# Memory layer: weighing in 32-row tiles, the surprise split between VectorE and Pool

## The chip, the cores and the metric

The program runs on one core of a Trainium2 chip. The metric is the device time of one execution in microseconds, as the median of three runs. Engines are named as in the profile: PE (TensorE; PEld are its weight loads), DVE (VectorE), ACT (ScalarE), POOL (GpSimd), SP (SyncE, which here only issues DMAs).

## The reference, cut to what matters

The reference is a stack of eight layers over x of 4 x 1024 x 128 in float32: four mixing layers, each followed by an expert layer. The change is in the seventh, a segment-wise memory attention with 16 heads of 64 and 32 segments of 32 tokens:

```python
def step(carry, inp):                      # one segment, all batches and heads
    mem, z = carry
    scores = where(mask, q_s @ k_s.T * SCALE, -inf)
    sdpa = softmax(scores) @ v_s
    sq, sk = elu1(qn_s), elu1(kn_s)        # q and k before the rotation
    mem_out = (sq @ mem) / (sq @ z + 1e-6)
    out = beta * mem_out + (1 - beta) * sdpa
    prev_v = (sk @ mem) / (sk @ z)
    mem = mem + sk.T @ (v_s - prev_v)      # v_s - prev_v: the surprise
    z = z + sk.sum(tokens)
```

then `out` times w_out is added to x.

## The kernel before, in words

`memory_layer` (L1845) walks 128 items j: 32 segments, and for each segment 4 groups of 4 heads. An item holds all 4 batches: 128 partitions are 4 batches x 32 tokens. Within an item the 4 heads are two pairs (index n or blk), each with an even and an odd head (parity, e).

Each engine has its program written out by hand: one loop over k, and in each round calls for different items, so that the items are pipelined. Engines meet by semaphores alone; each executes its queue in order.

- PE in round k: `score(k-2)` (L2092: q times k rotated), `prev(k-2)` (L2115: keys times memory), `lift_values(k)` (L2127: values of the new item), `weigh(k-4)` (L2104 and L2107), `num(k-2)` (L2120: queries times memory), `lift_keys(k)` (L2175: keys transposed), `project(k+1)` (L2138: q and k of the next item), one `product` (L2149: a finished output times w_out; four rounds make up one addition to x), `learn(k-3)` (L2168: the memory's update).
- DVE in round k: `remember(k-4)` (L2229: update taken off the memory), `sines(k)` (L2235), `cosines(k)` (L2240), `shares`, `scale_p` and `turn_p(k-3)` (L2244, L2248, L2254: softmax divided by its sum and turned over in 32x32 blocks), in every fourth round `add` (L2288), in some rounds row statistics (L2292, L2296), and `recall(k-2)`: scores masked (L2259), 1/z (L2261), maximum (L2263), the surprise as four instructions, one for each head (L2272: previous value times 1/z minus value), 1/denominator (L2275), and the memory's part of the output, `m1` (L2279).
- ACT in round k: `copy_out(k-4)` (L2041: the weighed output out of PSUM), `lift_out(k)` (L2065), `features(k+1)` (L2048, L2049, L2051), `recall(k-2)` (L2058: four exponentials).
- POOL in round k: `features(k)` (L2013), `spread(k-3)` (L2000), `rotate(k)` (L2007). SP sends the sines' product to the neighbouring partitions by two DMAs for each k (L1962, the `mates`); `rotate(k)` waits for them, `cosines(k+1)` waits for `rotate(k)`, since it overwrites its input.

`weigh` adds two things in PSUM: m1 turned over (a product with the identity), and values times probabilities. The four batches share the 128 partitions, so `spread` first lays the probabilities out as a 128x128 matrix for each head, which is zero outside of its batch's 32x32 block and holds the gate (1 - beta): 128x512 elements an item. `weigh` is then 2 matmuls of 128x128 and 4 matmuls of 128 rows by 64 columns, each over 128 columns. A float32 matmul makes two records in the profile. The 128x512 gate table `own_g` is made by POOL before the loop (L1978 to L1989).

`learn(j)` waits for the surprise of j, which `recall(j)` has finished one round before. `remember(j)`, the first of DVE's next round, waits for `learn(j)`.

Of the kernel before, what the change touches and what calls it, by code (L numbers as in the profile page):

```python
# [8 lines left out]
ALU = mybir.AluOpType  # L9
ACT = mybir.ActivationFunctionType  # L10
AX_X = mybir.AxisListType.X

P = 128
# [1831 lines left out]
def memory_layer(nc, g, wq, wk, wv, w_out, ln_g, ln_b, mem_beta, rope):  # L1845
# [11 lines left out]
    PR, NU, SC = 0, PB * E1, 2 * PB * E1  # L1857
    UP, OT = 4, 192
    N = W * NQ
    LEARNED = N - NQ  # L1860
    GROUP = 4 * NQ
    with ExitStack() as ctx:
# [22 lines left out]
        pe_, pn, pt = s.sb("pe_", [P, QH, SEG]), s.sb("pn", [P, QH, SEG]), s.sb("pt", [P, QH, SEG])  # L1885
        pt_e = s.sb("pt_e", [P, 2, QH, BATCH, SEG])
        own, share, own_g = s.sb("own", [P, BATCH, SEG]), s.sb("share", [P, H]), s.sb("own_g", [P, NQ, QH, BATCH, SEG])
        nm, sm, rs = s.sb("nm", [P, QH]), s.sb("sm", [P, 2, QH]), s.sb("rs", [P, QH])
# [5 lines left out]
        b_up = ps[:, UP:UP + BATCH, 0:PB * E1]  # L1894
        b_ot = ps[:, UP:UP + PB, OT:OT + P]
        b_out = ps[:, UP + 2:UP + 4, OT:OT + 2 * P].rearrange("p c (d f) -> p c d f", f=P)

        names = ("rows_loaded", "gate_loaded", "loaded", "made", "g_ready", "setup", "xn_ready", "turned", "xt_ready", "proj_ready", "t2_ready", "mates_even", "mates_odd",
                 "ab_used", "below_ready", "er_ready", "below_exp", "el_ready", "rope_ready", "lift_ready", "lifted", "scored", "recalled", "s1_ready", "rd_ready", "nm_ready",
                 "u_ready", "den_ready", "dn_ready", "m1_ready", "p_ready", "share_ready", "own_gated", "rsum_ready", "pn_ready", "pt_ready", "pte_ready",  # L1900
                 "upd_ready", "mem_ready", "weighed", "ot_copied", "out_ready", "x_ready", "stats")
# [43 lines left out]
        with nc.Block() as block:  # L1945
# [18 lines left out]
            @block.gpsimd  # L1964
            def _(pool):
                nc.gpsimd.memset(mask[:], 0.0).then_inc(S["made"], 1)
                for b in range(BATCH):
                    pool.wait_ge(S["made"], b + 1)
                    nc.gpsimd.affine_select(out=mask[32 * b:32 * b + 32], in_=mask[32 * b:32 * b + 32], compare_op=ALU.is_ge, fill=-1.0e30,
                                            base=0, pattern=[[0, PB], [-1, SEG]], channel_multiplier=1).then_inc(S["made"], 1)  # L1970
                pool.wait_ge(S["made"], 5)
                nc.gpsimd.memset(mem[:], 0.0).then_inc(S["made"], 1)
                pool.wait_ge(S["made"], 6)
                nc.gpsimd.memset(mem[:, :, :, :, D:E1], 1.0e-6).then_inc(S["made"], 1)
                pool.wait_ge(S["made"], 7)
                nc.gpsimd.memset(uu[:, :, :, D:E1], -1.0).then_inc(S["made"], 1)
                pool.wait_ge(S["made"], 8)
                nc.gpsimd.memset(own[:], 0.0).then_inc(S["made"], 1)  # L1978
                for b in range(BATCH):
                    pool.wait_ge(S["made"], 9 + b)  # L1980
                    nc.gpsimd.memset(own[SEG * b:SEG * b + SEG, b, :], 1.0).then_inc(S["made"], 1)
                pool.wait_ge(S["made"], 13)


                pool.wait_ge(S["share_ready"], 1)
                for q in range(NQ):
                    for e in range(2):
                        shape = [P, PB, BATCH, SEG]
                        gated = nc.gpsimd.tensor_tensor(own_g[:, q, e * PB:e * PB + PB], own[:].unsqueeze(1).to_broadcast(shape),  # L1989
                                                        share[:, q * QH + e:q * QH + QH:2].unsqueeze(2).unsqueeze(3).to_broadcast(shape), ALU.mult)  # L1990
                gated.then_inc(S["own_gated"], 1)
                pool.wait_ge(S["own_gated"], 1)

                def spread(j):

                    pool.wait_ge(S["pt_ready"], j + 1)
                    if j >= 2:
                        pool.wait_ge(S["weighed"], j - 1)
                    shape = [P, QH, BATCH, SEG]
                    nc.gpsimd.tensor_tensor(pt_e[:, j % 2], pt[:].unsqueeze(2).to_broadcast(shape), own_g[:, j % NQ], ALU.mult).then_inc(S["pte_ready"], 1)  # L2000

                def rotate(k):
                    if k >= 2:
                        pool.wait_ge(S["scored"], k - 1)
                    pool.wait_ge(S["ab_used"], k + 1)
                    pool.wait_ge(mates_ready[k % 2], 32 * (k // 2 + 1))
                    nc.gpsimd.tensor_tensor(rope_qk[:, k % 2].rearrange("p a b -> p (a b)"), t1[:], mates[:, k % 2, :], ALU.subtract).then_inc(S["rope_ready"], 1)  # L2007

                def features(k):
                    pool.wait_ge(S["below_exp"], k + 1)  # L2010
                    if k >= 3:
                        pool.wait_ge(S["recalled"], k - 2)
                    nc.gpsimd.tensor_tensor(el[:, k % 3].rearrange("p a b -> p (a b)"), ee[:], rr[:], ALU.add).then_inc(S["el_ready"], 1)  # L2013

                for k in range(N + 3):
                    if k < N:
                        features(k)
                    if 0 <= k - 3 < N:
                        spread(k - 3)
                    if k < N:  # L2020
                        rotate(k)

            @block.scalar
            def _(act):
# [11 lines left out]
                def copy_out(j):  # L2036
                    act.wait_ge(S["weighed"], j + 1)
                    w, q = j // NQ, j % NQ
                    if j >= 2 * GROUP and j % GROUP == 0:
                        act.wait_ge(S["out_ready"], 4 * NQ * (j // GROUP - 1))  # L2040
                    nc.scalar.activation(oT[:, w // 4 % 2, q * PB:q * PB + PB, :, w % 4, :], b_ot.rearrange("p n (b t) -> p n b t", t=SEG), ACT.Copy).then_inc(S["ot_copied"], 1)  # L2041

# [35 lines left out]
            def _(pe):  # L2078
# [16 lines left out]
                def weigh(j):  # L2095
# [4 lines left out]
                    if j:  # L2100
                        pe.wait_ge(S["ot_copied"], j)
                    pe.wait_ge(S["pte_ready"], j + 1)
                    for n in range(PB):
                        nc.tensor.matmul(ps[:, UP + n, OT:OT + P], m1[:, j % 2, 2 * n:2 * n + 2, :].rearrange("p h d -> p (h d)"), g.ident[:], start=True, stop=False, skip_group_check=True)  # L2104
                    for n in range(PB):
                        for e in range(2):
                            last = nc.tensor.matmul(ps[D * e:D * e + D, UP + n, OT:OT + P], values_of(j)[:, 2 * n + e, :], pt_e[:, j % 2, PB * e + n].rearrange("p b t -> p (b t)"),  # L2107
                                                    start=False, stop=True, skip_group_check=True)
                    last.then_inc(S["weighed"], 1)
# [31 lines left out]
                def product(k, p, b):  # L2141

                    i, first = parts[p]
                    pe.wait_ge(S["ot_copied"], GROUP * i + 3 * NQ + first // PB + 1)
                    pe.wait_ge(S["mem_ready"], min(k - 3, LEARNED))
# [31 lines left out]

                pe.wait_ge(S["made"], 13)
                for c in range(2 * BATCH):
# [28 lines left out]
            def _(dve):  # L2208
# [8 lines left out]
                dve.wait_ge(S["g_ready"], 1)  # L2217
                dve.wait_ge(S["made"], 13)
                nc.vector.tensor_scalar_add(gate[:, 1:3, :], gate[:, 1:3, :], 1.0).then_inc(S["setup"], 1)
# [30 lines left out]
                def turn_p(j):  # L2250
                    dve.wait_ge(S["pn_ready"], j + 1)
                    if j:
                        dve.wait_ge(S["pte_ready"], j)
                    nc.vector.transpose(pt[:].rearrange("p a b -> p (a b)"), pn[:].rearrange("p a b -> p (a b)")).then_inc(S["pt_ready"], 1)  # L2254

                def recall(j):
# [9 lines left out]
                                                   gate[:, 1, q * QH:q * QH + QH].rearrange("p (k e) -> p e k", e=2), ALU.add, ALU.mult).then_inc(S["den_ready"], 1)  # L2266
                    dve.wait_ge(S["lifted"], j + 1)
                    if 2 <= j < LEARNED:
                        dve.wait_ge(S["upd_ready"], j - 1)
                    for h in range(QH):  # L2270
                        e, n = h // PB, h % PB
                        last = nc.vector.scalar_tensor_tensor(uu[:, r, h, 0:D], prev_view[:, e, n, 0:D], rd[:, h:h + 1], values_of(j)[:, 2 * n + e, :], ALU.mult, ALU.subtract)  # L2272
                    last.then_inc(S["u_ready"], 1)
                    dve.wait_ge(S["den_ready"], j + 1)
# [23 lines left out]
                for k in range(N + 6):  # L2298
                    if 0 <= k - 4 < LEARNED:
                        remember(k - 4)  # L2300
                    if k < N:
                        sines(k)
# [4 lines left out]
                    if 0 <= k - 3 < N:  # L2307
                        scale_p(k - 3)
                        turn_p(k - 3)
                    if k in added_in:  # L2310
                        add(added_in[k])
                    if k - 1 in stats_in:
# [149 lines left out]
```

## Time and profile before

| | us |
|---|---|
| median of 3 runs | 2612.66 (2610.97 to 2617.28) |
| profiled execution: span from first to last instruction | 2623.8 |
| memory layer's loop: first and last L2000 start | 1769.6 and 2440.9 |
| busy over the whole span: PE, PEld, DVE, ACT, POOL | 2176.9, 1549.2, 1700.0, 1437.8, 1106.7 |

The profiled execution's own device time is not given apart from its span; the launch around the span is not in it, and the span alone is already 11.1 us over the median of the runs without a profile. A row of the timeline reads: start, duration, engine, line, operation, output<-input, shapes, how many instructions are merged, and in brackets the idle time in front and what ended it. In a windows row, the busy time of each engine in a stretch stands with its number of records.

### The profile page before, as it was taken

How to read it: one execution, taken by the hardware profiler on the slowest of the kernel's cores; microseconds unless marked ns; L12 is line 12 of the kernel's file. 1: busy time of each engine (PE TensorE's matmuls, PEld its weight loads, DVE VectorE, ACT ScalarE, POOL GpSimd, SP SyncE). 2: the span in 40 equal slices, each digit the busy share in tenths (PEclk: the TensorE clock that was granted, in tenths of full speed). 3: DMA queues.
4: the chain of work that ended last, by engine and by line, in shares of the span. 5: the costliest groups of instructions: out<-in, count | busy, mean ns of one | idle time of the engine just before them, and what ended most of it. 6: DMA issues, size and time to landing. Idle time of an engine off the chain costs nothing. (4 is left out here: it accounts for less than half of the span.)

```text
span 2623.8 us, 79243 instructions
## 1 busy us (share of the span) xinstructions
PE 2176.9 (83%) x30448; PEld 1549.2 (59%) x30448; DVE 1700.0 (65%) x5819; ACT 1437.8 (55%) x3704; POOL 1106.7 (42%) x1076
## 2 busy tenths in 40 slices
PE   6499948589964889899999977948999999999696
PEld 3288845379862233333334336937778777787396
DVE  6722247642336778787878833358999989899522
ACT  5455544355552256455455555537777767776353
POOL 2066644146654120120200004547777777776164
PEclk7699979789986799998989888969999999999798
DMA  4011120011125121111111000121111111111013
GB/s 133 33 42 43 43 85 2 33 32 44 43 93 163 55 58 31 38 39 31 35 46 35 5 33 29 41 85 54 54 53 56 52 53 55 52 56 52 35 42 92
DMA packets 76025, 134.96 MB, mean 51 GB/s; under 512 B 17225, under 2 KB 32264, under 8 KB 73224
## 3 DMA queue, kind: packets, MB, share of 16 engines
q1 hardware_dynamic: 62080, 102.07, 12.6%
q0 software_dynamic: 13568, 27.81, 3.7%
q8 instruction: 250, 4.10, 0.7%
q14 instruction: 119, 0.97, 0.1%
q10 hardware_dynamic: 8, 0.00, 0.0%
HBM read 65.19 MB, written 32.79 MB: 37 GB/s over the span
## 5 line engine op out<-in xcount | busy, mean ns | idle before, releaser
L1544 ACT ACTIVATE ca_pt<-ca_ps 128x512 f32<-128x512 f32 (+3 forms) x768 | 341.1, 491 | 322.3 <-PE ca_ps L1649 137.2
L734 PE MATMUL ffn_ps<-ffn_xst,ffn_up_w 128*128 128x128 f32 x3392 | 420.8, 278 | 0.2 <-issue 0.2
L734 PEld LDWEIGHTS ffn_ps<-ffn_xst,ffn_up_w 128*128 128x128 f32 x3392 | 402.9, 195 | 1.2 <-issue 1.2
L857 DVE TENSOR_TENSOR ffn_hid<-ffn_sg,ffn_ps 128x512 f32<-128x512 f32 x212 | 145.8, 688 | 359.2 <-PE ffn_ps L734 110.9
L576 POOL DMA_INDIRECT ffn_xs<-ffn_x,ffn_token_at x212 | 205.2, 968 | 301.5 <-DVE ffn_token_at L840 165.5
L581 POOL DMA_INDIRECT ffn_y<-ffn_ys,ffn_result_at x212 | 208.8, 985 | 139.2 <-DVE ffn_ys L863 82.3
L1645 PE MATMUL ca_ps<-ca_stacks 75*128 75x512 bf16 (+3 forms) x768 | 245.2, 342 | 18.3 <-ACT ca_pt L1544 10.7
L1777 DVE TENSOR_REDUCE ca_m_far<-ca_ps 128x1 f32<-128x128 f32 (+5 forms) x384 | 236.7, 616 | 30.3 <-PE ca_ps L1623 27.9
L643 ACT ACTIVATE ffn_sg<-ffn_ps 128x512 f32<-128x512 f32 x212 | 125.7, 593 | 233.6 <-remote 182.3
L1623 PE MATMUL ca_ps<-ca_stacks 72*128 72x512 bf16 (+3 forms) x768 | 223.4, 356 | 34.1 <-DVE ca_m_near L1778 21.9
L1778 DVE CUSTOM_DVE_ANT_0 ca_spill<-ca_ps,ca_bias_q 128x256 f32<-128x256 f32 (+1 forms) x512 | 201.1, 397 | 10.9 <-PE ca_ps L1623 10.9
L2000 POOL TENSOR_TENSOR im_pt_e<-im_pt,im_own_g 128x512 f32<-128x512 f32 x128 | 162.9, 1273 | 105.7 <-DVE im_pt L2254 105.7
L2007 POOL TENSOR_TENSOR im_rope_qk<-im_t,im_mates 128x512 f32<-128x512 f32 x128 | 163.1, 1275 | 65.4 <-DMA im_mates<-im_t 58.5
L1468 POOL TENSOR_TENSOR ca_full<-ca_rot 128x512 f32<-128x512 f32 x12 | 15.3, 1277 | 397.9 <-DVEq L1731 397.9
L742 PE MATMUL ffn_ps<-w_w,ffn_hid 128*128 x1136 | 158.0, 282 | 25.3 <-DVE ffn_ys L863 22.0
L2013 POOL TENSOR_TENSOR im_el<-im_ee,im_rr 128x512 f32<-128x512 f32 x128 | 162.9, 1273 | 34.7 <-ACT im_ee L2051 33.5
L1667 PE MATMUL ca_ps<-ca_pt,ca_vp 128*9 128x512 f32 (+3 forms) x1536 | 170.1, 516 | 0.0
L1623 PEld LDWEIGHTS ca_ps<-ca_stacks 72*128 72x128 bf16 x768 | 66.0, 101 | 164.9 <-DVE ca_m_near L1778 100.0
L742 PEld LDWEIGHTS ffn_ps<-w_w,ffn_hid 128*128 128x128 f32 x1136 | 137.7, 191 | 41.6 <-issue 39.9
L1645 PEld LDWEIGHTS ca_ps<-ca_stacks 75*128 75x128 bf16 x768 | 76.3, 100 | 138.3 <-ACT ca_pt L1544 86.3
L2058 ACT ACTIVATE im_pe_<-im_s,im_nm 128x32 f32<-128x32 f32 x512 | 156.9, 315 | 1.9 <-DVE im_nm L2263 1.9
L650 ACT ACTIVATE ffn_up_w<-w_w 128x1024 f32 x142 | 150.4, 1060 | 11.0 <-DVE ffn_table_e L829 3.6
(340 smaller groups left out, 4742.0 us busy)
## 6 DMA issues: line engine op xcount, KB each, us to landing
im_mates<-im_t SPq DMA_DIRECT2D x256, 128.0 KB
ffn_got<-ffn_y SPq DMA_DIRECT2D x48, 256.0 KB, 5.8
ca_stacks<-scratch_q_piece SPq DMA_DIRECT2D x16, 576.0 KB
ca_stacks<-scratch_k_piece SPq DMA_DIRECT2D x48, 192.0 KB
ffn_x<-ffn_xn SPq DMA_DIRECT2D x32, 256.0 KB, 2.0
w_w<-in_L_ffn_experts_w_dram SPq DMA_DIRECT2D x2, 2048.0 KB, 12.0
ffn_xs<-ffn_x,ffn_token_at POOLq DMA_INDIRECT x212
ffn_y<-ffn_ys,ffn_result_at POOLq DMA_INDIRECT x212
```

Of the source, the lines that this page charges most:

```text
L576: nc.gpsimd.indirect_dma_start(out=xs[:, n % XS, :], out_offset=None, in_=xn_rows[:, :], in_offset=bass.IndirectOffsetOnAxis(ap=token_at[: ...
L581: nc.gpsimd.indirect_dma_start(out=y_rows[:, :], out_offset=bass.IndirectOffsetOnAxis(ap=result_at[:, n:n + 1], axis=0), in_=ys[:, n % YS, ...
L734: last = nc.tensor.matmul(ps[:, bank, j * P:j * P + P], up_w[:, n % WS, first + j * P:first + j * P + P], xst[:, n % 2, :], start=True, st ...
L742: last = nc.tensor.matmul(ps[:, 5, 0:P], hid[:, n % 2, j * P:j * P + P], down(e, j), start=(j == 0), stop=(j == IB - 1))
L1544: nc.scalar.activation(pt[:, i % 8, lo - c0:hi - c0], ps[:, tile_bank(i), lo - c0:hi - c0], ACT.Exp, scale=SCALE).then_inc(p_ready, 1)
L1623: last = nc.tensor.matmul(slot_row(n)[:, c:e], stacks[0:KD, u % 3, 0, j, qt * P:qt * P + P], stacks[0:KD, u % 3, 1, j, c:e], start=True, s ...
L1645: last = nc.tensor.matmul(ps[:, tile_bank(i), lo - c0:hi - c0], stacks[:, u % 3, 1, j, kt * P:kt * P + P], stacks[:, u % 3, 0, j, lo:hi], ...
L1667: nc.tensor.matmul(ps[32 * j:32 * j + D + 1, 7, lo - c0:hi - c0], vp[:, b % 2, kt, gr * G4 + j, :], pt[:, i % 8, lo - c0:hi - c0], start=( ...
L1777: nc.vector.tensor_reduce(m_far[:, u % 2, t:t + 1], slot_row(n)[:, 0:lo], AX_X, ALU.max)
L1778: nc.vector.tensor_tensor_reduce(spill[:, n % 2, 0:hi - lo], slot_row(n)[:, lo:hi], bias_q[:, h, W2 - (hi - lo):W2], 1.0, NEG, ALU.add, AL ...
L2000: nc.gpsimd.tensor_tensor(pt_e[:, j % 2], pt[:].unsqueeze(2).to_broadcast(shape), own_g[:, j % NQ], ALU.mult).then_inc(S["pte_ready"], 1)
L2007: nc.gpsimd.tensor_tensor(rope_qk[:, k % 2].rearrange("p a b -> p (a b)"), t1[:], mates[:, k % 2, :], ALU.subtract).then_inc(S["rope_ready ...
```

## The change

1. `weigh`: m1 and the values are no longer used across all 128 partitions. For each pair n there are 8 matmuls with the identity's 32x32 block and 8 matmuls with the probabilities, each of 32 rows (one batch), 64 columns (one head) and 32 columns of data: 32 matmuls an item in the place of 6. The output now lies in four PSUM banks (one a batch) and not in two.
2. `spread` becomes `gate_p`: one 128x128 multiplication by the gate. The table `own_g` and its making fall away; four small copies of the shares take its place. The number that PE and DVE wait for at the start goes from 13 memsets to 8.
3. The surprise: DVE makes previous value times 1/z for all four heads in one instruction (128x256, broadcast); POOL's new `surprise(k-3)`, between `gate_p(k-3)` and `rotate(k)`, subtracts the values in place (128x256) and releases `learn`.
4. `add` moves within DVE's round from behind `turn_p` to behind `remember`; `weigh` waits for it, and `product` waits for the `copy_out` of the same round, since output and products now share two banks.

```diff
+        pt_g = s.sb("pt_g", [P, 2, QH, SEG])
+        share, sorted_share = s.sb("share", [P, H]), s.sb("sorted_share", [P, NQ, QH])
-        b_ot = ps[:, UP:UP + PB, OT:OT + P]
-        b_out = ps[:, UP + 2:UP + 4, OT:OT + 2 * P].rearrange("p c (d f) -> p c d f", f=P)
+        b_ot = ps[:, UP:UP + BATCH, OT:OT + PB * SEG]
+        b_out = ps[:, UP + 2:UP + 4, OUT:OUT + 2 * P].rearrange("p c (d f) -> p c d f", f=P)
...
+                for q in range(NQ):
+                    gated = nc.gpsimd.tensor_copy(sorted_share[:, q]..., share[:, q * QH:q * QH + QH]...)
-                def spread(j):
+                def gate_p(j):
                     pool.wait_ge(S["pt_ready"], j + 1)
                     if j >= 2:
                         pool.wait_ge(S["weighed"], j - 1)
-                    shape = [P, QH, BATCH, SEG]
-                    nc.gpsimd.tensor_tensor(pt_e[:, j % 2], pt[:].unsqueeze(2).to_broadcast(shape), own_g[:, j % NQ], ALU.mult).then_inc(S["pte_ready"], 1)
+                    nc.gpsimd.tensor_tensor(pt_g[:, j % 2], pt[:], bl(sorted_share[:, j % NQ], SEG), ALU.mult).then_inc(S["ptg_ready"], 1)
+                def surprise(j):
+                    pool.wait_ge(S["known"], j + 1)
+                    pool.wait_ge(S["lifted"], j + 1)
+                    new = pairs(uu[:, j % 2, :, 0:D])
+                    nc.gpsimd.tensor_tensor(new, new, sorted_heads(values_of(j)), ALU.subtract).then_inc(S["u_ready"], 1)
...
                     if 0 <= k - 3 < N:
-                        spread(k - 3)
+                        gate_p(k - 3)
+                    if 0 <= k - 3 < LEARNED:
+                        surprise(k - 3)
                     if k < N:
                         rotate(k)
...
                     if j:
                         pe.wait_ge(S["ot_copied"], j)
-                    pe.wait_ge(S["pte_ready"], j + 1)
+                    if adds_by[j + 4]:
+                        pe.wait_ge(S["x_ready"], adds_by[j + 4])
+                    pe.wait_ge(S["ptg_ready"], j + 1)
                     for n in range(PB):
-                        nc.tensor.matmul(ps[:, UP + n, OT:OT + P], m1[...], g.ident[:], start=True, stop=False)
-                    for n in range(PB):
-                        for e in range(2):
-                            last = nc.tensor.matmul(ps[D * e:D * e + D, UP + n, OT:OT + P], values_of(j)[:, 2 * n + e, :], pt_e[...], start=False, stop=True)
+                        heads = [(b, e, slice(SEG * b, SEG * b + SEG), ps[D * e:D * e + D, UP + b, OT + SEG * n:OT + SEG * n + SEG]) for b in range(BATCH) for e in range(2)]
+                        for b, e, tok, out in heads:
+                            nc.tensor.matmul(out, m1[tok, j % 2, 2 * n + e, :], g.ident[tok, tok], start=True, stop=False)
+                        for b, e, tok, out in heads:
+                            last = nc.tensor.matmul(out, values_of(j)[tok, 2 * n + e, :], pt_g[tok, j % 2, PB * e + n, :], start=False, stop=True)
...
-                    pe.wait_ge(S["ot_copied"], GROUP * i + 3 * NQ + first // PB + 1)
+                    pe.wait_ge(S["ot_copied"], min(k - 3, N))
...
-                    dve.wait_ge(S["lifted"], j + 1)
                     if 2 <= j < LEARNED:
                         dve.wait_ge(S["upd_ready"], j - 1)
-                    for h in range(QH):
-                        e, n = h // PB, h % PB
-                        last = nc.vector.scalar_tensor_tensor(uu[:, r, h, 0:D], prev_view[:, e, n, 0:D], rd[:, h:h + 1], values_of(j)[:, 2 * n + e, :], ALU.mult, ALU.subtract)
-                    last.then_inc(S["u_ready"], 1)
+                    nc.vector.tensor_tensor(pairs(uu[:, r, :, 0:D]), prev_view[:, :, :, 0:D], over(rd[:], D), ALU.mult).then_inc(S["known"], 1)
...
                     if 0 <= k - 4 < LEARNED:
                         remember(k - 4)
+                    if k in added_in:
+                        add(added_in[k])
                     if k < N:
                         sines(k)
...
                         turn_p(k - 3)
-                    if k in added_in:
-                        add(added_in[k])
```

## Rows read from the trace of the kernel before

**Rows 1.** Instructions of one tile (the probabilities laid out): duration min/median/max ns, first and last start
```profile
L2000 POOL TENSOR_TENSOR im_pt_e<-im_pt,im_own_g x128: 1262/1272/1285, 1769.6 to 2440.9; 128x512 f32<-128x512 f32 x128
```
**Rows 2.** Windows: stretch, length; PE, PEld, DVE, ACT, POOL busy; clock, DMA share, GB/s
```profile
2000.00:2100.00 100.00, 94.44 (x2948) 79.84 (x2947) 91.34 (x317) 71.72 (x247) 71.98 (x57) 1.00 0.16 54
```
**Rows 3.** Timeline, one round of PE (start us, us, engine, line, what)
```profile
2044.75 0.36 PE L2092 MATMUL im_ps<-im_rope_qk 64*32 64x32 f32 x32
...
2044.97 0.58 PE L2115 MATMUL im_ps<-im_mem,im_el 64*32 64x65 f32 x32
...
2046.02 0.61 PE L2104 MATMUL im_ps<-g_ident,im_m 128*128 128x128 f32 x4
...
2047.14 0.46 PE L2120 MATMUL im_ps<-im_mem,im_el 64*32 64x65 f32 x32
...
2047.54 0.44 PE L2175 MATMUL im_ps<-g_ident,im_el 128*128 128x128 f32 x2
...
2049.24 0.49 PE L2168 MATMUL im_ps<-im_uu,im_lift 32*64 32x65 f32 x32
```
**Rows 4.** Timeline, DVE and POOL of the same rounds
```profile
2042.62 0.29 DVE L2259 SCALAR_TENSOR_TENSOR im_s<-im_ps,im_mask 128x128 f32<-128x128 f32 x1
...
2043.21 0.85 DVE L2272 SCALAR_TENSOR_TENSOR im_uu<-im_ps,im_rd,im_lift 128x64 f32<-128x64 f32 x4
...
2044.13 0.49 PE L2168 MATMUL im_ps<-im_uu,im_lift 32*64 32x65 f32 x32
2044.18 0.42 DVE L2279 TENSOR_TENSOR im_m<-im_ps,im_dn 128x256 f32<-128x256 f32 x1
...
2044.74 0.70 DVE L2229 TENSOR_TENSOR im_mem<-im_mem,im_ps 128x520 f32<-128x520 f32 x1
...
2045.36 0.68 DVE L2235 TENSOR_TENSOR im_t<-im_ps,im_cs 128x512 f32<-128x512 f32 x1
2045.96 0.68 DVE L2240 TENSOR_TENSOR im_t<-im_ps,im_cs 128x512 f32<-128x512 f32 x1
...
2047.41 0.65 DVE L2288 TENSOR_TENSOR g_x<-g_x,im_ps 128x512 f32<-128x512 f32 x1
...
2047.56 1.28 POOL L2000 TENSOR_TENSOR im_pt_e<-im_pt,im_own_g 128x512 f32<-128x512 f32 x1 [0.82 <-DVE im_pt L2254]
...
2050.26 1.28 POOL L2007 TENSOR_TENSOR im_rope_qk<-im_t,im_mates 128x512 f32<-128x512 f32 x1 [1.42 <-DMA im_mates<-im_t]
```
**Rows 5.** Timeline, the same, one round earlier
```profile
2040.20 0.68 DVE L2235 TENSOR_TENSOR im_t<-im_ps,im_cs 128x512 f32<-128x512 f32 x1
...
2042.03 0.46 PE L2120 MATMUL im_ps<-im_mem,im_el 64*32 64x65 f32 x32
...
2043.64 1.26 POOL L2007 TENSOR_TENSOR im_rope_qk<-im_t,im_mates 128x512 f32<-128x512 f32 x1
```
**Rows 6.** Waits in the loop (1770 to 2440): engine line <- what: us, times, longest
```profile
POOL im_rope_qk L2007 <- DMA im_mates<-im_t: 55.3, 57, 2.2
...
DVE im_t L2240 <- POOL im_rope_qk L2007: 14.0, 23, 1.0
```
**Rows 7.** DMA queues of the span: packets, MB, share of 16 engines
```profile
q8 instruction: 250, 4.10, 0.7%
```
**Rows 8.** POOL's groups by shape: busy us, mean ns, idle in front
```profile
L1989 POOL TENSOR_TENSOR im_own_g<-im_own,im_share 128x256 f32<-128x256 f32 x8 | 4.6, 612 | 12.1 <-DVE im_share L2221 12.1
...
L975 POOL TENSOR_SCALAR lm_kk<-lm_ek,lm_rs 128x128 f32<-128x128 f32 x32 | 19.3, 604 | 44.7 <-DVE lm_rs L1125 42.2 <-PE lm_ps_t L1045 2.1
```
**Rows 9.** Timeline, the layer's start
```profile
1733.00 0.15 POOL L1976 MEMSET im_uu<- 128x8 f32 x1
...
1734.50 1.97 PE L2184 MATMUL im_ps<-g_ident,im_xn 128*128 128x128 f32 x8 [26.48 <-POOL im_own L1981]
...
1751.18 1.26 POOL L2013 TENSOR_TENSOR im_el<-im_ee,im_rr 128x512 f32<-128x512 f32 x1
```
**Rows 10.** Timeline, the layer's end
```profile
2444.53 2.05 PE L2149 MATMUL im_ps<-im_wo,im_ot 128*128 128x128 f32 x16
```

More of the change, by code:

```diff
@@ L1857, in memory_layer @@
     PR, NU, SC = 0, PB * E1, 2 * PB * E1
-    UP, OT = 4, 192
+    UP, OT, OUT = 4, 192, 256
     N = W * NQ
@@ L1885, in memory_layer @@
         pe_, pn, pt = s.sb("pe_", [P, QH, SEG]), s.sb("pn", [P, QH, SEG]), s.sb("pt", [P, QH, SEG])
-        pt_e = s.sb("pt_e", [P, 2, QH, BATCH, SEG])
-        own, share, own_g = s.sb("own", [P, BATCH, SEG]), s.sb("share", [P, H]), s.sb("own_g", [P, NQ, QH, BATCH, SEG])
+        pt_g = s.sb("pt_g", [P, 2, QH, SEG])
+        share, sorted_share = s.sb("share", [P, H]), s.sb("sorted_share", [P, NQ, QH])
         nm, sm, rs = s.sb("nm", [P, QH]), s.sb("sm", [P, 2, QH]), s.sb("rs", [P, QH])
@@ L1894, in memory_layer @@
         b_up = ps[:, UP:UP + BATCH, 0:PB * E1]
-        b_ot = ps[:, UP:UP + PB, OT:OT + P]
-        b_out = ps[:, UP + 2:UP + 4, OT:OT + 2 * P].rearrange("p c (d f) -> p c d f", f=P)
+        b_ot = ps[:, UP:UP + BATCH, OT:OT + PB * SEG]
+        b_out = ps[:, UP + 2:UP + 4, OUT:OUT + 2 * P].rearrange("p c (d f) -> p c d f", f=P)
         names = ("rows_loaded", "gate_loaded", "loaded", "made", "g_ready", "setup", "xn_ready", "turned", "xt_ready", "proj_ready", "t2_ready", "mates_even", "mates_odd",
                  "ab_used", "below_ready", "er_ready", "below_exp", "el_ready", "rope_ready", "lift_ready", "lifted", "scored", "recalled", "s1_ready", "rd_ready", "nm_ready",
-                 "u_ready", "den_ready", "dn_ready", "m1_ready", "p_ready", "share_ready", "own_gated", "rsum_ready", "pn_ready", "pt_ready", "pte_ready",
+                 "known", "u_ready", "den_ready", "dn_ready", "m1_ready", "p_ready", "share_ready", "share_sorted", "rsum_ready", "pn_ready", "pt_ready", "ptg_ready",
                  "upd_ready", "mem_ready", "weighed", "ot_copied", "out_ready", "x_ready", "stats")
@@ L1977, in _ @@
                 pool.wait_ge(S["made"], 8)
[L1978 to L1982, printed above, removed]
                 pool.wait_ge(S["share_ready"], 1)
                 for q in range(NQ):
-                    for e in range(2):
[L1988 to L1992, printed above, removed]
-                def spread(j):
+                    gated = nc.gpsimd.tensor_copy(sorted_share[:, q].rearrange("p (e k) -> p k e", e=2), share[:, q * QH:q * QH + QH].rearrange("p (k e) -> p k e", e=2))
+                gated.then_inc(S["share_sorted"], 1)
+                pool.wait_ge(S["share_sorted"], 1)
+                def gate_p(j):
                     pool.wait_ge(S["pt_ready"], j + 1)
@@ L2040, in copy_out @@
                         act.wait_ge(S["out_ready"], 4 * NQ * (j // GROUP - 1))
-                    nc.scalar.activation(oT[:, w // 4 % 2, q * PB:q * PB + PB, :, w % 4, :], b_ot.rearrange("p n (b t) -> p n b t", t=SEG), ACT.Copy).then_inc(S["ot_copied"], 1)
+                    nc.scalar.activation(oT[:, w // 4 % 2, q * PB:q * PB + PB, :, w % 4, :], b_ot.rearrange("p b (n t) -> p n b t", t=SEG), ACT.Copy).then_inc(S["ot_copied"], 1)
                 def features(k):
@@ L2101, in weigh @@
                         pe.wait_ge(S["ot_copied"], j)
-                    pe.wait_ge(S["pte_ready"], j + 1)
+                    if adds_by[j + 4]:
+                        pe.wait_ge(S["x_ready"], adds_by[j + 4])
+                    pe.wait_ge(S["ptg_ready"], j + 1)
                     for n in range(PB):
-                        nc.tensor.matmul(ps[:, UP + n, OT:OT + P], m1[:, j % 2, 2 * n:2 * n + 2, :].rearrange("p h d -> p (h d)"), g.ident[:], start=True, stop=False, skip_group_check=True)
-                    for n in range(PB):
-                        for e in range(2):
-                            last = nc.tensor.matmul(ps[D * e:D * e + D, UP + n, OT:OT + P], values_of(j)[:, 2 * n + e, :], pt_e[:, j % 2, PB * e + n].rearrange("p b t -> p (b t)"),
-                                                    start=False, stop=True, skip_group_check=True)
+                        heads = [(b, e, slice(SEG * b, SEG * b + SEG), ps[D * e:D * e + D, UP + b, OT + SEG * n:OT + SEG * n + SEG]) for b in range(BATCH) for e in range(2)]
+                        for b, e, tok, out in heads:
+                            nc.tensor.matmul(out, m1[tok, j % 2, 2 * n + e, :], g.ident[tok, tok], start=True, stop=False, skip_group_check=True)
+                        for b, e, tok, out in heads:
+                            last = nc.tensor.matmul(out, values_of(j)[tok, 2 * n + e, :], pt_g[tok, j % 2, PB * e + n, :], start=False, stop=True, skip_group_check=True)
                     last.then_inc(S["weighed"], 1)
@@ L2176, in lift_keys @@
                     last.then_inc(S["lift_ready"], 1)
-                pe.wait_ge(S["made"], 13)
+                pe.wait_ge(S["made"], 8)
                 for c in range(2 * BATCH):
@@ L2217, in _ @@
                 dve.wait_ge(S["g_ready"], 1)
-                dve.wait_ge(S["made"], 13)
+                dve.wait_ge(S["made"], 8)
                 nc.vector.tensor_scalar_add(gate[:, 1:3, :], gate[:, 1:3, :], 1.0).then_inc(S["setup"], 1)
@@ L2252, in turn_p @@
                     if j:
-                        dve.wait_ge(S["pte_ready"], j)
+                        dve.wait_ge(S["ptg_ready"], j)
                     nc.vector.transpose(pt[:].rearrange("p a b -> p (a b)"), pn[:].rearrange("p a b -> p (a b)")).then_inc(S["pt_ready"], 1)
```

## The prediction

> **What bounds the kernel now.** I read in this order: one tile's instructions, for the length of a round; the windows, for what is full; the timeline of two rounds, for who waits for whom; the waits, for the transfers. L2000 starts 128 times between 1769.6 and 2440.9, so a round takes 671.3 / 127 = 5.29 us [rows 1]. In a window of 100 us inside, PE is busy 94.4 and DVE 91.3, ACT and POOL 72 each, the clock 1.00 [rows 2]: PE and DVE are both nearly full, and neither alone says what a cut is worth. The timeline does.
>
> Loop A goes through both. From `score` (2044.75) to `num` (2047.14) is 2.39 us of PE [rows 3]; from `num` to the masking of scores 0.59 (2042.03 [rows 5] to 2042.62), from there to the end of m1 1.98 (2044.18 + 0.42 - 2042.62), and m1's end to the next `score` 0.15 [rows 3, 4]. Sum 5.11. Both large edits lie in it: `weigh` between score and num, the four surprise instructions between masking and m1.
>
> PE alone: 2044.75 to 2049.24, and 0.50 for `learn` [rows 3]: 4.99. DVE alone: 91.3 busy in 100 us is 0.913 x 5.29 = 4.83 [rows 1, 2]. The rest from 5.11 to 5.29 are two things: `add` (0.65 in one round of four, 0.16 a round [rows 4]) and the transfers. The sines' product (2040.20 + 0.68) is rotated 2.76 us after its end in one round; in the next (2045.36 + 0.68) 4.22 us after, 1.42 of it waiting for the DMA [rows 4, 5]. This time, X below, is 2.8 when undisturbed; with the 55.3 us of rotate's waits over 126 rounds its mean is 2.8 + 0.4 = 3.2 or somewhat more (POOL is still busy in a part of it). DVE lost only 14.0 us to it [rows 6].
>
> **Part 1, `weigh` in tiles.** Now 2046.02 to 2047.14, 1.12 us for 6 matmuls [rows 3]. Afterwards 32 matmuls, 64 records. The nearest rows are `score` and `learn`, 16 matmuls (32 records) each. Score has the same 32 columns of data with 32-column weights and takes 0.22 until the next group starts (2044.97); learn has the same 32-row, 64-column weights but 65 columns of data, and takes 0.50. Twice each: 0.44 to 1.00. I take 0.70, nearer to learn because its weight shape is the same. PE saves 0.42 (0.12 to 0.68).
>
> The undisturbed rate of small matmuls is the row's: 0.22 us / 32 records = 7 ns. The Trainium skill says otherwise for a single one: "TensorEngine Tiling (Array Packing)", section Instruction Overhead, puts about 60 cycles on each matmul however few its columns. At 2.4 GHz that is an estimate of 25 ns for each of 64 records, 1.6 us, 0.5 slower than now, and a round would be bound by PE.
>
> **Part 2, POOL.** The making of the table goes (see the ends). In the loop a 128x512 multiplication of 1.27 us [rows 1] becomes one of 128x128 and one of 128x256. For 256 columns there is a row, 0.61; 512 to 256 falls by 0.66, so 128 would be 0.30; the upper bound for it is another form of 128x128 at 0.60 [rows 8]. Gate 0.30 (0.25 to 0.60), surprise 0.65 (0.61 to 1.27, in place and with reordered heads). POOL's sum falls by 0.3 a round.
>
> **Part 3, the surprise.** DVE's four instructions took 0.85; one with a broadcast and 256 columns from PSUM has a twin in m1, 0.42 [rows 4]. DVE saves 0.43. The Trainium skill, "GPSIMD Reference", section 4.1, speaks against the other half: two-input elementwise work is about twice as slow on GpSimd and belongs on VectorE. The trace agrees (128x512 in 1.27 on POOL, 0.68 on DVE [rows 4]). By that rule the subtraction stays on DVE: DVE alone would then be 4.83 a round, and by the rows of the loops it is 4.40 for DVE and 4.45 for the loop through POOL.
>
> What this moves: the surprise was ready one round ahead. Now it waits for `turn_p` of the same round and two POOL instructions, and behind the waiting `learn` stand all of PE's queue, the next `score`, `prev`, `weigh`. Loop B is new. From rows: learn to remember 0.61 (2044.13, 2044.74), to sines 0.62, to cosines 0.60, to the gate's start 1.60 (2047.56) [rows 4]; then 0.30 + 0.65 and 0.07 for the hand-over: 4.45.
>
> **Part 4, `add` and the waits.** In front of the sines, `add` (0.65) lies in loop B: 0.16 a round, as much as before in loop A; no gain, no loss. PE's wait for it in `weigh`: remember starts 0.61 after learn, add ends 0.7 + 0.65 later, at 1.96; `weigh` starts 0.5 + 1.27 = 1.77 after learn, so 0.2 in one round of four, below loop B's slack. `product` waits for a copy that takes 0.4 behind `weigh`; `num` (0.40 from 2047.14 to 2047.54 [rows 3]), `lift_keys` and `project` (8 records of a kind of which 16 take 2.05 [rows 10], so 1.0) hide it. If that cover were gone it would cost 0.5.
>
> **What is late next.** Loop A falls to 5.11 - 0.42 - 0.43 = 4.26; PE alone to 4.57; DVE alone to 4.40 and some gaps; loop B is 4.45, 4.61 with `add`. But the transfers now have less to hide behind. After learn the sines end at 1.91; plus X, rotate 1.28 and features 1.27 (POOL in order), 0.05, and from `lift_keys` to the learn after next 1.70 (2047.54 to 2049.24) [rows 3, 4, 9]: 6.2 + X over two rounds. Before, at 5.11 a round, X could reach 4.0 at no cost. Now at 4.5 it may be 2.8: every disturbed transfer costs. With X = 3.3 a round is 4.75; with the 4.22 of the row 5.2. A mean of waits is above the wait of a mean, `add` brings 0.16, and PE's instructions grow: 2948 + 2947 records in 100 us are 312 a round, and 104 are added, by a third; the instruction queue's 250 packets took 0.7% of 16 engines' span, 2623.8 x 16 x 0.007 / 250 = 1.2 us each [rows 7], and may fall on a transfer more often. I take 0.1 for the last, and so 5.0 us a round.
>
> **Sum.** Rounds: 120 full ones x (5.29 - 5.00) = 35. Start: PE waited for the memsets until 1734.50 and could go at 1733.2, 1.3; the first features stood until 1751.18 behind the table (612 ns x 8 = 4.9), four small copies at 0.15 to 0.2 (a memset of 8 columns is 0.15) leave 3.8 [rows 8, 9]: 5 in all. End: in the last three rounds `weigh` waits for an addition (0.65) and `product` for a copy, while a product is 2.05 long [rows 10]: 0.65 + 0.4 in three rounds is 3 lost, with nothing else to do for PE, and 0.4 to 0.7 a round is given back by the faster `weigh` and by additions that end earlier: say 1 lost. Together 39: the span of 2623.8 becomes 2585. The medians lie 11 under the profiled span, and I keep that distance: 2573 us.
>
> **Rivals.**
> - *The loops close, the transfers don't bind (2532).* The undisturbed X of 2.76 is in one of two rows, and shorter rounds may shift the collisions. Then loop B or PE with `add` is the bound, 4.65 a round: 0.64 x 120 + 4 = 81 off. Against: 57 of 126 rotates wait already.
> - *The transfers hold the round (2601).* X stays at 3.9 to 4.2 in most rounds as instruction packets multiply: 5.2 to 5.25 a round, 0.07 x 120 + 4 = 12 off. For: the row of 4.22. Against: half of the rounds wait for nothing.
> - *Slower: learn through POOL and late transfers (2640).* The mechanism is the 6.2 + X above, or loop B with POOL's upper bounds (4.45 + 0.30 + 0.62 = 5.37, with `add` 5.53). It decides from a mean X of 4.4, or from 5.13 in loop B without `add`. With 5.55: 0.26 x 120 - 4 = 27 on. For: X of 4.2 to 5.0 exists (the longest wait is 2.2 [rows 6], X = 5.0). Against: the rows of POOL scale with columns.
> - *Slower: small matmuls don't overlap (2650).* Four groups of 8 write the same places in turn. If each must drain first (score's row lasts 0.36, the next group starts after 0.22: 0.14 each [rows 3]) on top of the upper 1.00, `weigh` takes 1.56, PE alone 5.43, with waits 5.6: 0.31 x 120 = 37 on. Against: score and learn overlap theirs. The Trainium skill's "TensorEngine Tiling (Array Packing)", as above, would give nearly the same. This is also the case in which the change doesn't do what it says.
>
> **How the numbers follow.** Forecast (2550 to 2595, its own range) 0.60; loops close 0.14; transfers hold 0.11; slower through POOL 0.08, through small matmuls 0.02; 0.05 for no change out of cancelling errors. 0.3% is 7.8 us, about what a measurement tells from no change: faster is below 2605, slower above 2620. Faster 0.60 + 0.14 + 0.11 = 0.85, same 0.05, slower 0.10. The range reaches from 4.70 a round (2538) to 5.25 (2604): with the unknown prices of `weigh` and POOL at their bounds both ends are in reach.
>
> **What would show it.** The new weigh groups end 0.6 to 0.8 after they start; the single DVE product 0.42; POOL's two near 0.30 and 0.65, without idle time between them; PE waits at `learn` for POOL, or at `lift_keys` for features, where now it waits at `score` for m1; rotate's waits for the DMA grow from 55 us towards 80 or more; masking on DVE waits less for PE. The prediction is wrong if PE shows a round over 5.2 with `weigh` over 1.0, if POOL's surprise takes over 1 us, or if rotate hardly waits.

## The result and the profile after

The changed kernel takes 2766.05 us (2761.42 to 2792.0, 4 runs) against 2614.97 (4 runs): a ratio of 1.060 (95% interval 1.055 to 1.065), 151 us slower. The forecast was 2573 us, faster, with a range of 2538 to 2604. The profiled execution has a span of 2759.2 us, 135.4 more than before.

The first lines answer to [rows 1] and [rows 2]: POOL's gating with its first and last start, and the window of 100 us.

```profile
L1991 POOL TENSOR_TENSOR im_pt_g<-im_pt,im_sorted_share x128: 400/401/403, 1751.4 to 2568.6; 128x128 f32<-128x128 f32 x128
```

```profile
2000.00:2100.00 100.00, 82.23 (x3213) 67.42 (x3201) 67.40 (x210) 58.64 (x205) 54.60 (x62) 0.93 0.13 44
```

A round is now (2568.6 - 1751.4) / 127 = 6.43 us, where it was 5.29. Over the loop this is 817.2 against 671.3, 145.9 us more, of 135.4 for the whole span: all of the loss is in the rounds. Yet every compute engine is less busy than before: PE 82 for 94, DVE 67 for 91, POOL 55 for 72. No engine's work bounds the round. Only the number of PE records per 100 us has risen, from 2948 to 3213.

Next PE's own timeline in the changed kernel, one round and a half. It answers to [rows 3].

```profile
2044.21 0.49 PE L2170 MATMUL im_ps<-im_uu,im_lift 32*64 32x65 f32 x32
2044.63 0.28 PE L2092 MATMUL im_ps<-im_rope_qk 64*32 64x32 f32 x14
2045.54 0.28 PE L2092 MATMUL im_ps<-im_rope_qk 64*32 64x32 f32 x15 [0.63 <-issue]
2045.63 0.22 PE L2117 MATMUL im_ps<-im_mem,im_el 64*32 64x65 f32 x1
2045.64 0.19 PE L2092 MATMUL im_ps<-im_rope_qk 64*32 64x32 f32 x1
2045.64 0.22 PE L2117 MATMUL im_ps<-im_mem,im_el 64*32 64x65 f32 x1
2045.65 0.19 PE L2092 MATMUL im_ps<-im_rope_qk 64*32 64x32 f32 x1
2045.65 0.23 PE L2117 MATMUL im_ps<-im_mem,im_el 64*32 64x65 f32 x2
2045.66 0.19 PE L2092 MATMUL im_ps<-im_rope_qk 64*32 64x32 f32 x1
2045.67 0.57 PE L2117 MATMUL im_ps<-im_mem,im_el 64*32 64x65 f32 x28
2046.17 0.70 PE L2129 MATMUL im_ps<-im_wv,im_xt_all 128*128 128x256 f32 x2
2046.80 0.34 PE L2108 MATMUL im_ps<-g_ident,im_m 32*64 32x32 f32 x16
2046.93 0.32 PE L2110 MATMUL im_ps<-im_pt_g,im_lift 32*64 32x32 f32 x16
2047.06 0.40 PE L2108 MATMUL im_ps<-g_ident,im_m 32*64 32x32 f32 x12
...
2047.31 0.34 PE L2110 MATMUL im_ps<-im_pt_g,im_lift 32*64 32x32 f32 x12
2047.58 0.32 PE L2122 MATMUL im_ps<-im_mem,im_el 64*32 64x65 f32 x11
2049.26 0.65 PE L2122 MATMUL im_ps<-im_mem,im_el 64*32 64x65 f32 x21 [1.35 <-issue]
2049.83 0.69 PE L2177 MATMUL im_ps<-g_ident,im_el 128*128 128x128 f32 x2
2050.31 1.92 PE L2140 MATMUL im_ps<-im_xt_all,im_w 128*128 128x128 f32 x8
```

PE stops twice in the middle of a group: after 14 of the 32 records of `score` (next record at 2045.54, 0.63 idle), and after 11 of the 32 of `num` (1.35 idle). No semaphore stands there: the waits are in front of a group, and the profile names "issue". Count the matmul records between the two stops: 15, then 35 up to 2045.67 (1 + 1 + 1 + 1 + 2 + 1 + 28), 2 of the values, 64 of `weigh` (eight of them are not shown), 11 of `num`: 127, and as many weight loads, 254 instructions. Between most other neighbouring stops there are 125 to 127 matmul records, or two or three times as many. A stop is counted where more than 0.45 us pass between the starts of two neighbouring matmul records of one group. In 116 rounds there are 121 of them, 141 us from record to record; before there were 3.

No fixed price on each instruction does this either: the 128 records of `weigh`, weight loads included, take 0.78 us here, 6 ns each, while the round as a whole needs 15.

`weigh` itself, the step I was least sure of, is as forecast: 2046.80 to 2047.58, 0.78 us for 0.70.

Now the instruction queue, in 400 us inside the loop (1900 to 2300): before, then after, packets and MB and share of 16 engines, with the windows row of the same stretch.

```profile
q8 instruction: 94, 1.54, 1.7%
...
1900.00:2300.00 400.00, 377.85 (x11778) 318.61 (x11777) 362.84 (x1267) 286.03 (x979) 285.98 (x227) 1.00 0.16 54
```

```profile
q8 instruction: 101, 1.65, 1.8%
...
1900.00:2300.00 400.00, 331.70 (x12809) 272.56 (x12808) 267.70 (x841) 234.14 (x804) 219.41 (x246) 0.93 0.13 45
```

A packet is 1.65 MB / 101 = 16 KB. After, 25,617 PE records came in 101 packets, 254 each; before, 23,555 in 94, 251 each. This queue carries PE's instructions in blocks of about 256, so an instruction is 64 bytes. A block takes 400 / 101 = 3.96 us after and 4.26 before. These are means: in the changed kernel single packets start 3.3 to 5.9 us apart. A round holds 208 matmul records and as many weight loads after (156 and 156 before): 416 / 254 blocks x 3.96 = 6.5 us.

The packets' own times tie the stops to this queue. The packet that starts at 2046.62 takes 1.25 us and ends at 2047.86; PE, whose last record before the stop started at 2047.69, goes on at 2049.26, 1.39 us after that end. So it is nearly everywhere: 116 of 120 stops in the changed kernel and 110 of 111 in `work` (below) end 1.2 to 1.6 us after the end of a packet, by the median 1.39. The next packet starts 1.3 us (median) after PE has gone on, and takes 1.0. These three stretches follow one another, 3.7 of the 3.9 us.

The Trainium skill, "Runtime: NRT & Kernel Launch", section Instruction fetch mechanics, says that instructions come in blocks of 256 and the next is fetched while one runs, and that the fetch is hidden because the sequencer dispatches more slowly than it is refilled. The trace agrees on the block (254 records a packet) and not on the hiding: here PE stands still until 1.39 us after the packet has landed.

### The profile page after: what moved, and what is told of

Read it like the earlier page. It is cut to its first block and busy times, and to the rows that moved or that the text cites. A ratio compares the mean times of both kernels' runs of the same rounds, so it can differ in the third digit from the quotient of the medians.

```text
span 2759.2 us, 92288 instructions
## 1 busy us (share of the span) xinstructions
PE 2218.2 (80%) x37104; PEld 1574.6 (57%) x37104; DVE 1640.4 (59%) x5435; ACT 1436.8 (52%) x3704; POOL 1073.9 (39%) x1191
## 5 line engine op out<-in xcount | busy, mean ns | idle before, releaser
L2231 DVE TENSOR_TENSOR im_mem<-im_mem,im_ps 128x520 f32<-128x520 f32 x124 | 86.3, 696 | 135.3 <-PE im_ps L2170 134.6
L2140 PE MATMUL im_ps<-im_xt_all,im_w 128*128 128x128 f32 x1024 | 159.9, 307 | 3.4 <-issue 2.6
```

## The experiments

Theory F: blocks of about 256 instructions do not reach PE faster than one in about 3.9 us on the mean, so a round is at least (records / 254) x 3.9, whatever the work. Rivals: L, `learn` waits for POOL; M, PE's work on small matmuls; X, the transfers of the rotation. The kernel before, run beside each experiment, takes 2559 to 2602 us there and not 2615, so ratios are compared. That difference is not in this layer's rounds as far as can be seen: from first to last gating tiles_only takes 817.1 us, the changed kernel 817.2. Rounds are first to last start of L1991 or its twin, over 127, from one profiled execution each; stops are counted as above.

| kernel | records a round | round us | stops | q8 blocks in 400 us | ratio (95%) |
|---|---|---|---|---|---|
| before | 312 | 5.29 | 3 | 94 | 1 |
| changed | 416 | 6.43 | 121 | 101 | 1.060 (1.055 to 1.065) |
| tiles_only | 416 | 6.43 | 108 | 103 | 1.056 (1.051 to 1.062) |
| surprise_first | 416 | 6.40 | 116 | 103 | 1.055 (1.050 to 1.059) |
| no_mates | 416 | 6.35 | 118 | 104 | 1.053 (1.048 to 1.057) |
| work | 424 | 6.50 | 111 | 102 | 1.062 (1.057 to 1.067) |
| wide_ident | 384 | 6.01 | 62 | 101 | 1.040 (1.033 to 1.046) |
| score2 | 376 | 5.99 | 59 | 99 | 1.034 (1.030 to 1.039) |
| values_only | 352 | 5.53 | 86 | 101 | 1.012 (1.008 to 1.016) |
| split_last | 312 | 5.48 | 10 | 90 | 1.009 (1.006 to 1.012) |
| split_first | 312 | 5.24 | 12 | 93 | 0.996 (0.993 to 0.999) |
| best | 312 | 5.16 | 3 | 96 | 0.997 (0.995 to 0.999) |

**tiles_only**: the tiles kept, the surprise back on DVE.

```diff
-                        surprise(k - 3)
...
-                    nc.vector.tensor_tensor(pairs(uu[:, r, :, 0:D]), prev_view[...], over(rd[:], D), ALU.mult).then_inc(S["known"], 1)
+                    dve.wait_ge(S["lifted"], j + 1)
+                    for h in range(QH):
+                        e, n = h // PB, h % PB
+                        last = nc.vector.scalar_tensor_tensor(uu[:, r, h, 0:D], prev_view[:, e, n, 0:D], rd[:, h:h + 1], values_of(j)[:, 2 * n + e, :], ALU.mult, ALU.subtract)
+                    last.then_inc(S["u_ready"], 1)
```

> The changed kernel with the surprise back on DVE, as four instructions released one round ahead; POOL only gates the probabilities. Theory F (PE's instruction stream): PE's instructions arrive in blocks of 16 KB, and a block takes about 3.9 us to arrive whatever is in it; a round holds about 416 matmul and weight-load records and cannot be shorter than 416 / 256 x 3.95 = 6.4 us. The count is unchanged, so the time stays at 2766, within 12. Rival L (the surprise through POOL holds `learn`): the wait is gone, so the round returns to 5.3 or less, 2620 or less. Rival M (small matmuls are themselves slow): as F for the time, but without gaps inside a group of matmuls.

1.056, its interval overlapping that of the changed kernel, and the same round of 6.43: F. Without the new wait the loss stays, so L explains almost none of it. The changed kernel's own trace says so too: between 1780 and 2500 `learn` (L2170) waited for POOL's subtraction 4 times, 1.9 us in all.

**score2**: in the kernel before, 64 more records of very little work.

```diff
+                    for again in range(2):
+                        last = for_heads(...)   # cut: the scores' 16 matmuls
+                    last.then_inc(S["scored"], 1)
```

> The kernel before with the 16 matmuls of the scores issued twice, same result: 32 matmuls, 64 records, 0.22 us of PE more in a round. Theory F: 376 to 384 records, so a round of 5.8 to 5.95 and 2685 to 2700, with gaps inside groups as in the changed kernel. Rival M or L: only the work counts, at most 0.22 x 128 = 28 more, 2641 or less, no gaps.

1.034, 88 us for 28 at most by M, and a little above the 1.027 to 1.033 that F gave (2685 to 2700 for 2615). The unchanged design, given more instructions, slows as the changed one does. The stops are there: its group L2117 waits for "issue" within (1800 to 2300).

```profile
POOL im_rope_qk L2007 <- DMA im_mates<-im_t: 43.5, 40, 2.3
...
PE im_ps L2117 <- issue: 26.9, 28, 1.7
```

**work**: in the changed kernel, much more work and few instructions.

```diff
+                    for again in range(3):
                         nc.tensor.matmul(b_lift[:, 0:QH * D], XT[:, k // NQ, :], wv_s[...], start=True, stop=True)
```

> The changed kernel with the matmul of the values (256 columns, 0.54 us) issued three times, same result: 1.07 us of PE work more in a round, but only 8 records. Theory F: 8 / 256 x 3.95 = 0.12 a round, 15 in all: 2781, within 15. Rival M (PE's work bounds the changed kernel): 1.07 x 128 = 137 more, 2900. Rival L: something between, since `learn` waits for POOL anyway.

1.062 (after: 1.060), where M asked for about 1.11. Its window of 400 us:

```profile
1900.00:2300.00 400.00, 354.18 (x12855) 291.66 (x12844) 265.60 (x836) 230.28 (x788) 216.65 (x243) 1.00 0.13 44
```

PE is busy 354 us for 332 with nearly the same number of records (12,855 for 12,809). The idle time that the blocks leave takes up the work. M falls. Mind the clock: 1.00 here, 0.93 in the changed kernel, at the same time a round.

**split_first and split_last**: the kernel before with only the surprise split; POOL's part ahead of, or behind, the laying out of the probabilities.

```diff
                     if 0 <= k - 3 < LEARNED:
+                        surprise(k - 3)          # split_first
                     if 0 <= k - 3 < N:
                         spread(k - 3)
+                        surprise(k - 3)          # split_last
```

> The kernel before (weighing as 6 matmuls, probabilities laid out by POOL) with the surprise as one product on DVE and the subtraction on POOL, placed ahead of the laying out. Theory F: 312 records a round as before, floor 4.8 us, so no gaps inside groups; DVE is relieved by 0.43 and PE alone is 4.99, so a round of 5.1 to 5.3: 2585 to 2613. Rival L: the subtraction on POOL costs by itself, 2640 or more. Rival M expects the same as F here.

> The kernel before with the surprise split between DVE and POOL, POOL's part behind its laying out (in the order of the changed kernel). No more PE instructions than before. Loop B by its rows: 0.61 + 0.62 + 0.60 + 1.60 + 1.27 + 0.68 + 0.07 = 5.45 a round without the addition, against 5.29 measured with it before. Theory L as a mechanism: slower than before by 0.15 x 124 = 19 us or more, ratio 1.007 or more, where the same kernel with POOL's part first had 0.996. If `learn` has slack: 0.996 again.

0.996 and 1.009. The split is a small gain (the interval ends at 0.999), and its place decides: behind the 1.27 us instruction, `learn` waits for POOL in nearly every round. The waits of split_last (1800 to 2300):

```profile
PEld im_ps L2177 <- POOL im_uu L2007: 48.0, 80, 0.9
...
PE im_ps L2177 <- POOL im_uu L2007: 32.8, 79, 0.7
```

Its round, 5.48, is what loop B gave with the longer POOL instruction (5.45). Loop B is real; in the changed kernel, with the gate at 0.40, it is shorter, and the blocks' 6.4 lies above it.

**surprise_first**: the changed kernel with that order.

> The changed kernel with POOL's subtraction ahead of its gating, so that `learn` no longer waits for the turned probabilities of the same round. Theory F (blocks of PE's instructions, 423 in a round): unchanged, 1.055 to 1.062 of the kernel before, with over 100 gaps inside groups of matmuls. Rival L (the new wait of `learn`): 1.00 or less.

1.055: L had asked for 1.00. The interval overlaps that of the changed kernel (1.055 to 1.059 is common to both), and the round is 6.40 for 6.43; at most about 0.5% could belong to the wait.

**wide_ident**: 24 matmuls in the place of 32.

```diff
-                        for b, e, tok, out in heads:
-                            nc.tensor.matmul(out, m1[tok, j % 2, 2 * n + e, :], g.ident[tok, tok], start=True, stop=False)
+                        for b in range(BATCH):
+                            nc.tensor.matmul(ps[:, UP + b, OT + SEG * n:OT + SEG * n + SEG], m1[tok, j % 2, 2 * n:2 * n + 2, :]..., g.ident[tok, tok], start=True, stop=False)
```

> The changed kernel with the identity part of `weigh` taken for two heads at a time: 32 rows by 128 columns, 8 matmuls for 16, 24 matmuls in all. Theory F: 32 instructions fewer of 423 in a round, 32 x 15.4 ns = 0.49 us, 63 us of the 152: ratio 1.035 (1.03 to 1.04), as the kernel with the scores issued twice, which has nearly the same count. Rival M (PE's work): 16 records at 11 ns, 0.09 to 0.18 a round less, ratio 1.05 to 1.056.

1.040, at the edge of what F gave; M had 1.05 to 1.056, above the measured interval. The round fell by 0.43, for 0.49 expected. Its round is 6.01, that of score2 5.99: two kernels of different design with nearly the same count.

**no_mates**: no transfers beside the instructions.

```diff
-                    for odd in range(2):
-                        sp.dma_start(mates[...], t2[...]).then_inc(mates_ready[k % 2], 16)
+                    sp.sem_inc(mates_ready[k % 2], 32)
...
-                    nc.gpsimd.tensor_tensor(rope_qk[...], t1[:], mates[:, k % 2, :], ALU.subtract).then_inc(S["rope_ready"], 1)
+                    nc.gpsimd.tensor_tensor(rope_qk[...], t1[:], t2[:, k % 2, :], ALU.subtract).then_inc(S["rope_ready"], 1)
...
-                        dve.wait_ge(mates_ready[k % 2], 32 * (k // 2))
+                        dve.wait_ge(S["rope_ready"], k - 1)
```

> The changed kernel without the DMAs that exchange neighbouring partitions for the rotation: the rotation reads its own partition's product, so the output is another. All DMA left in the loop is instructions. Theory F: the count of PE's instructions is the same; if a block's arrival does not depend on the transfers beside it, the time stays at 1.05 to 1.06; if the transfers delay it, the round falls in part, to 1.02 to 1.05, and the time per block with it. Rival X (late transfers of the rotation bound the round): 1.00 or less.

```profile
q8 instruction: 104, 1.70, 1.7%
...
1900.00:2300.00 400.00, 336.76 (x13067) 277.04 (x13051) 273.27 (x867) 238.51 (x819) 221.43 (x251) 0.93 0.02 5
```

The DMA share falls from 0.13 to 0.02, the block from 3.96 to 3.85 us, the round from 6.43 to 6.35, the ratio to 1.053. X falls, and the traffic beside it makes at most 3% of the block's time.

**values_only**: the identity part of `weigh` left out, 64 records fewer; the values' matmuls stay and now start the sum themselves.

```diff
-                        for b, e, tok, out in heads:
-                            nc.tensor.matmul(out, m1[tok, j % 2, 2 * n + e, :], g.ident[tok, tok], start=True, stop=False)
```

> The changed kernel with the identity part of `weigh` left out (the memory's part is missing from the output): 16 matmuls, 64 instructions fewer, 359 of 423 left in a round. Theory F: the floor is 359 / 256 x 3.92 = 5.50 us a round, 0.93 less than the changed kernel, ratio 1.01 (1.005 to 1.02), gaps inside groups down to 20 to 50. Rival M (PE's work bounds): 0.2 to 0.35 a round less, ratio 1.04 or more.

1.012 and 5.53, as expected; but 86 stops, not 20 to 50: the blocks still bind, with shorter waits. `weigh` takes 0.39 us of PE here (median from its start to the start of `num`), for 1.12 in the kernel before, and the kernel is still slower than that one: it has 40 records more a round.

**best**: split_first, with the gate table made after POOL's first round, PE and DVE waiting for 8 memsets.

```diff
+                    if k == 0:
+                        lay_gates()
...
-                pe.wait_ge(S["made"], 13)
+                pe.wait_ge(S["made"], 8)
```

> The kernel before with the surprise split, POOL's subtraction first, and the gate table made by POOL after its first round instead of ahead of it, PE and DVE waiting for 8 memsets and not 13. The start of the layer is 5 us shorter (1.3 and 3.8 by the rows of before), the rounds are those of the split kernel (0.996): ratio 0.994 (0.991 to 0.996). If the start was hidden behind the first transfers: 0.996.

0.997 (0.995 to 0.999), 0.3% faster than before, above the 0.991 to 0.996 expected and not told apart from split_first. The gain at the layer's start does not show in the ratio.

## Why the prediction was wrong

The step that failed is "What is late next", in its words on the instructions: "PE's instructions grow ... by a third; the instruction queue's 250 packets ... may fall on a transfer more often. I take 0.1". I had the count right and the wrong victim. The packets are PE's own supply; the sum counted the 1.2 us that one takes as a burden on other transfers, and had no term for PE waiting for it. A block takes 3.85 to 4.04 us in every kernel that is short of instructions, and no sum of durations shows it. What the runs put in the place of 0.1 is a floor of 6.4 us a round, 1.4 over the 5.00 of the forecast, 178 us over 127 rounds. [rows 2] held the rate, 5895 records in 100 us, 23 blocks, 4.3 us a block, but not the limit: that the kernel before ran within a tenth of it (4.26 for 3.9) could be known only once starved kernels had been measured. Whether the rounds would have come to 5.0 without that floor is not shown. There is a hint against it: split_first, with DVE's saving of 0.43 alone and no stops to speak of, went from 5.29 to 5.24 only.

None of the prediction's own signs of being wrong was met: the round was over 5.2, but with `weigh` at 0.78, the surprise at 0.68 and a rotate that waited. Two forecast signs failed: PE at `learn` hardly ever waited for POOL, and masking on DVE waited more for PE, not less (L2261, 95.2 us between 1780 and 2500; L2259 before, 28.6 between 1770 and 2440).

The rest, point by point:

- **`weigh` in tiles**: 0.70 forecast, 0.78 measured; PE's own work fell as said. The rival "small matmuls don't overlap (2650)" had the sign and not the mechanism: they overlap (6 ns a record), and just by that PE eats a block faster than the next arrives.
- **POOL**, measured (forecast): gate 0.40 (0.30, range 0.25 to 0.60), surprise 0.68 (0.65). **DVE**: the product 0.42 (0.42). The rows of the changed kernel, 1900 to 2300:

```profile
L1998 POOL TENSOR_TENSOR im_uu<-im_uu,im_lift 128x256 f32<-128x256 f32 x61 | 41.7, 684 | 0.0
...
L2271 DVE TENSOR_TENSOR im_uu<-im_ps,im_rd 128x256 f32<-128x256 f32 x61 | 25.3, 415 | 0.0
L1991 POOL TENSOR_TENSOR im_pt_g<-im_pt,im_sorted_share 128x128 f32<-128x128 f32 x61 | 24.4, 401 | 61.0 <-DVE im_pt L2256 61.0
```

- **Loop B**: 4.45 forecast for the changed kernel; not to be seen there, as the blocks' floor lies above it, but shown by split_last against split_first.
- **Transfers**: the forecast sign, rotate's waits growing from 55 us "towards 80 or more", came (1780 to 2500):

```profile
DVE im_mem L2231 <- PE im_ps L2170: 121.2, 108, 3.6
...
POOL im_rope_qk L2005 <- DMA im_mates<-im_t: 85.2, 89, 2.4
```

  It was a sign of something else: no_mates takes the transfers away and the round falls by 0.08 of its 1.14 us of loss. With the 6.2 + X loop I had built a second story on waits of an engine off the path.
- **Start**: 5 us forecast. From the layer's first memset to the first gating it is 33.4 us after (1717.97 to 1751.37) and 40.4 before (1729.14 to 1769.56): 7.0 gained, 4.3 of them up to the first features (1717.97 to 1735.71, before 1729.14 to 1751.18). One term of the 5 was added wrongly: 4.9 less four copies at 0.15 to 0.2 is 4.1 to 4.3, not 3.8; the four copies took 0.56 together. The first lines of the layer's start after, for [rows 9]:

```profile
1717.97 0.16 POOL L1966 MEMSET im_mask<- 128x64 f32 x1 [7.29 <-POOLq L42]
...
1722.34 2.05 PE L2186 MATMUL im_ps<-g_ident,im_xn 128*128 128x128 f32 x8 [25.25 <-DVE im_xn L2217]
...
1734.07 0.56 POOL L1982 COPY im_sorted_share<-im_share 128x4 f32<-128x4 f32 x4 [12.08 <-DVE im_share L2223]
...
1735.71 1.26 POOL L2011 TENSOR_TENSOR im_el<-im_ee,im_rr 128x512 f32<-128x512 f32 x1 [1.07 <-ACT im_ee L2051]
```

- **End**: 1 us lost forecast. From the last gating to the end of the last addition 16.8 us (2568.6 to 2585.4), before 9.3 (2440.9 to 2450.2): 7.5 lost. The new waits are serial, as said, but most of the loss is the clock: between 2550 and 2557 PE was busy 2.73 of 7 us, from 2557 on the granted clock was 0.50, and it stayed there to the last product. At that level 16 records of a product take 3.78 us, for 2.05 at 1.00 in [rows 10]; the last three products make 5.2 of the 7.5 by it.

```profile
2576.22 3.78 PE L2151 MATMUL im_ps<-im_wo,im_ot 128*128 128x128 f32 x16 [0.48 <-ACT im_ot L2041]
2580.04 0.69 DVE L2286 TENSOR_TENSOR g_x<-g_x,im_ps 128x512 f32<-128x512 f32 x1 [5.72 <-PE im_ps L2151]
```

Also wrong was how the parts were tied: range and chances rested on terms of one kind, durations and waits, so a limit of another kind lay outside of all of them at once.

Open: what triggers a packet, and why PE needs 1.39 us after it has landed. Shown is only that packet, pause and the start of the next follow one another, and that neither the traffic beside them nor PE's work sets the 3.9 us. Open too is whether the kernel before loses by it; it ran at 4.26 us a block with 3 long stops.

## What to carry to other kernels

Count the instructions per microsecond, not only the busy time: where the records of matmuls and weight loads together near 65 a microsecond over a whole block of 256, more small matmuls cost 15 ns each record (3.9 us / 254) whatever they compute, and larger work can be free: in `work` 1.07 us more of PE in a round cost no more than its 8 records. By these runs, splitting matmuls into tiles to save array time pays only below that rate. Gaps inside a group of instructions, with "issue" as their reason, no semaphore in front and a constant number of instructions between them, or a multiple of it, are the sign.

## What the runs showed that was not expected

- Behind some of the long stops the granted clock falls. In the changed kernel the stretch before the stop of 2047.69 had 1.00; behind it 0.50, the 1.2 GHz level:

```profile
2044.00:2047.60 3.60, 2.97 (x168) 2.21 (x166) 2.26 (x5) 2.68 (x11) 1.98 (x3) 1.00 0.12 40
...
2049.30:2052.00 2.70, 2.70 (x31) 2.53 (x32) 1.52 (x7) 0.60 (x1) 1.84 (x2) 0.50 0.03 6
```

  The 8 records of `project` span 1.92 us there and 1.06 by the median of all rounds. It is not every stop: of the changed kernel's 120, 22 have a clock at or near 0.50 in the 1.5 us behind them, and `work`, with 111 stops and more work between them, runs at 1.00. In the loop the lower clock cost nothing that can be seen, since `work` is as slow without it.
- Eight kernels (the changed one, tiles_only, surprise_first, no_mates, work, wide_ident, score2, values_only) whose rounds differ by up to 1 us (5.53 to 6.50) take in 99 to 104 blocks in 400 us.
